# Gathering eight chosen slots by indirect DMA in place of a masked product over all 512 slots

## What is computed

```python
query = h @ Wq.T                              # h: layernorm of x, 64 numbers a token
rq, rk = query @ Wr.T, aux_keys @ Wr.T
router_scores = rq @ rk.T / sqrt(48) + log_rel           # 512 slots
top_scores, top_idx = top_k(router_scores, 8)
attn = (query . aux_keys[top_idx]) / sqrt(64) + log_rel[top_idx]
w = softmax(attn)
aux_out = (sum_k w_k * aux_values[top_idx_k]) @ Wvd.T @ Wvu.T
return h + gate * aux_out                     # gate: a sigmoid of an uncertainty
```

## Time and profile before

| what | value |
|---|---|
| median of 3 runs | 1070.32 us (1070.15 to 1070.88) |
| the profiled execution | 1074.47 us |
| its span, first to last instruction | 1072.6 us |
| TensorE busy | 97% of the span |
| VectorE, ScalarE, GpSimd busy | 74%, 52%, 17% |
| mean granted TensorE clock | 0.987 of full speed |

### The profile page before, as it was taken

One profiled execution on the slowest core, in us unless ns is written; L12 is line 12 of the kernel. 1 busy time (PEld: TensorE's weight loads), 2 busy tenths in 40 slices (PEclk: granted clock), 3 DMA queues, 4 the chain that ended last, 5 costly groups with the idle time before them and its releaser, 6 DMA issues. The chain is left out here.

```text
span 1072.6 us, 19294 instructions
## 1 busy us (share of the span) xinstructions
PE 1041.0 (97%) x6778; PEld 997.1 (93%) x6778; DVE 791.6 (74%) x1841; ACT 561.6 (52%) x881; POOL 183.4 (17%) x355
## 2 busy tenths in 40 slices
PE   6998999999999999999999999999999996999997
PEld 6998999998999999999999999999999995888885
DVE  4889646366758787787777787786877777788785
ACT  3643678544635545454554545454554554555553
POOL 0007000000002222313232222312232231000000
PEclk9999899999999999999999999999999997999999
DMA  8555557689379864744354734347352527999999
GB/s 241 157 155 193 196 212 291 246 295 280 94 219 242 218 176 117 214 110 125 92 142 115 196 98 123 112 112 214 98 142 79 151 62 228 402 409 412 403 422 371
DMA packets 109617, 218.96 MB, mean 204 GB/s; under 512 B 48388, under 2 KB 64804, under 8 KB 95528
## 3 DMA queue, kind: packets, MB, share of 16 engines
q1 hardware_dynamic: 99784, 180.68, 55.8%
q10 hardware_dynamic: 9216, 33.56, 7.9%
q0 software_dynamic: 576, 4.19, 0.9%
HBM read 174.10 MB, written 54.79 MB: 213 GB/s over the span
## 5 line engine op out<-in xcount | busy, mean ns | idle before, releaser
L56 PE MATMUL tk_bank<-b_weights,k_turned 128*128 128x384 f32 (+2 forms) x1056 | 348.8, 330 | 1.5 <-DVE b_weights L889 1.4
L58 PE MATMUL tk_bank<-b_weights,k_turned 128*128 128x384 f32 (+2 forms) x1056 | 339.9, 322 | 0.0
L57 PE MATMUL tk_bank<-b_weights,k_turned 128*128 128x384 f32 (+2 forms) x1056 | 339.7, 322 | 0.0
L56 PEld LDWEIGHTS tk_bank<-b_weights,k_turned 128*128 128x128 f32 x1056 | 198.6, 188 | 4.7 <-DVE b_weights L889 1.6
L57 PEld LDWEIGHTS tk_bank<-b_weights,k_turned 128*128 128x128 f32 x1056 | 198.8, 188 | 1.3
L58 PEld LDWEIGHTS tk_bank<-b_weights,k_turned 128*128 128x128 f32 x1056 | 198.3, 188 | 0.0
L1487 DVE STREAM_TRANSPOSE tk_bank<-k_rows 128x512 f32<-128x512 f32 x128 | 133.7, 1069 | 9.1 <-DMA k_rows<-in_x_dram 8.9
L1273 ACT ACTIVATE k_turned<-tk_bank 128x512 fp32r<-128x512 f32 x124 | 71.2, 594 | 73.9 <-DVE tk_bank L1487 73.5
L1897 DVE TENSOR_TENSOR late_x<-late_x,ob_out 128x512 f32<-128x512 f32 x96 | 65.8, 688 | 24.0 <-PE ob_out L58 22.6
L1497 DVE TENSOR_TENSOR k_turned<-tk_bank,k_turned 128x512 fp32r<-128x512 f32 x124 | 79.8, 686 | 0.9
L56 PE MATMUL tk_bank<-k_turned,a_T 128*128 128x256 f32 x256 | 76.1, 297 | 4.4 <-DVE a_T L343 3.9
(11 more groups left out here) (259 smaller groups left out, 2262.0 us busy)
## 6 DMA issues: line engine op xcount, KB each, us to landing
k_rows<-in_x_dram SPq DMA_DIRECT2D x40, 1024.0 KB, 4.8
k_rows<-in_x_dram SPq DMA_DIRECT2D x128, 256.0 KB, 5.2
late_x<-in_x_dram SPq DMA_DIRECT2D x24, 1024.0 KB, 8.3
out_dram<-late_x ACTq DMA_DIRECT2D x48, 512.0 KB, 14.1
k_rows<-in_Wq_dram SPq DMA_DIRECT2D x16, 1024.0 KB, 4.9
k_rows<-in_Wk_dram SPq DMA_DIRECT2D x9, 1024.0 KB, 4.8
out_dram<-k_rows ACTq DMA_DIRECT2D x16, 512.0 KB, 11.4
k_rows<-in_Wk_dram SPq DMA_DIRECT2D x28, 256.0 KB, 5.3
```

The lines of the kernel that those rows point to most:

```text
L56: pe.matmul(out, lh, rh, start=start, stop=False, skip_group_check=skip)
L57: pe.matmul(out, lh, rl, start=False, stop=False, skip_group_check=skip)
L58: return pe.matmul(out, ll, rh, start=False, stop=stop, skip_group_check=skip)
```

## The change

The masked row of 512 goes, with its exponential, its transposes, its product by `av` and the 512 key-dot columns of `late_route`. In their place `late_slots` ends with `max_index`, which gives eight indices per token. POOL gathers for each of the eight (`gather`, L1431) one row of 193 numbers per token out of a table in HBM (128 value numbers, 64 key numbers, the log relevance), with an indirect DMA of 128 rows. VectorE multiplies the gathered keys by the query and sums (`slot_dots`), ScalarE takes eight exponentials and scales the eight value rows (`slot_exp`, `slot_weigh`), VectorE adds them up (`slot_sum`). The table is written in the preparation. Four of the eight DMAs stand ahead of `first_mean`, four behind it. The iteration's order on VectorE also changes: `turn_x(t+1, 0)` moves ahead of `late_scale`, and `late_slots` ahead of `turn_x(t+1, 3)`; the polynomial of the activation moves to ScalarE. The slots of the last two tiles are finished in the output block, whose load into the buffer shared with the gathered rows waits for `z_out`.

```diff
 def load_slots(sp, io, scr, keep):
...
+    sp.dma_start(scr["table"][:, VB:VB + BOT], io["aux_keys"]).then_inc(keep["table_in"], 16)
+    sp.dma_start(scr["table"][:, VB + BOT:ROW], io["log_rel"].rearrange("(n a) -> n a", a=1),
+                 allow_slow_non_contiguous=True).then_inc(keep["table_in"], 16)
...
+def slot_dots(dve, keep, t, u):
+    rows = keep["slot_rows"][u].rearrange("p (k r) -> p k r", r=ROW)
+    own = rows[:, :, VB:VB + BOT]
+    query = keep["query_of"][u].unsqueeze(1).broadcast_to([P, TOPK, BOT])
+    dve.wait_ge(keep["gathered"][u], 16 * TOPK * (t // 2 + 1))
+    dve.tensor_tensor(own, own, query, ALU.mult)
+    dve.drain()
+    dve.tensor_reduce(keep["slot_dots"], own, AX.X, ALU.add)
+    dve.drain()
+    dve.scalar_tensor_tensor(keep["slot_scores"], keep["slot_dots"], -1.0 / float(BOT) ** 0.5,
+                             rows[:, :, VB + BOT:ROW].rearrange("p k o -> p (k o)"), ALU.mult, ALU.subtract)
+    dve.drain()
+    dve.tensor_reduce(keep["slot_max"], keep["slot_scores"], AX.X, ALU.min).then_inc(keep["nearest"], 1)
+def slot_weigh(act, keep, t, u):
+    act.wait_ge(keep["slot_exp"], t + 1)
+    for k in range(TOPK):
+        values = rows[:, k, 0:VB]
+        ins = act.activation(values, values, ACT.Copy, scale=keep["slot_weights"][:, k:k + 1])
+def slot_sum(dve, keep, t, u, late=False):
+    dve.wait_ge(keep["weighed"], t + 1)
+    dve.tensor_tensor(values[:, 0:4, :], values[:, 0:4, :], values[:, 4:8, :], ALU.add)
+    dve.drain()
+    dve.tensor_tensor(values[:, 0:2, :], values[:, 0:2, :], values[:, 2:4, :], ALU.add)
+    dve.drain()
+        dve.tensor_tensor(z, values[:, 0, :], values[:, 1, :], ALU.add).then_inc(keep["z_out"], 1)
...
 def late_route(t):
-                for bank_, n in ((psR, 0), (psS, NSLOT)):
-                    pe.matmul(bank_[:], qS[:], rs1[:, n:n + NSLOT], start=True, stop=False)
-                    ins = pe.matmul(bank_[:], q2s[0:BOT + 2, :], rs2[:, n:n + NSLOT], start=False, stop=True)
-            def late_turn_w(t):
-            def late_z(t, last=False):
+                pe.matmul(psR[:], qS[:], rs1[:], start=True, stop=False)
+                pe.matmul(psR[:], q2s[0:BOT + 2, :], rs2[:], start=False, stop=True).then_inc(S["routed"], 1)
...
@@ POOL
+            def gather(t, u, ks):
+                if ks[0] == 0:
+                    pool.drain()
+                    pool.wait_ge(S["slots"], t + 1)
+                    past(pool, keep["z_out"], t - 1)
+                    pool.tensor_tensor(issued[:], keep["eps"][:], keep["eps"][:], ALU.mult)
+                for k in ks:
+                    pool.indirect_dma_start(keep["slot_rows"][u][:, k * ROW:(k + 1) * ROW], None, scr["table"][:, :],
+                                            bass.IndirectOffsetOnAxis(ap=picked[u][:, k:k + 1], axis=0)
+                                            ).then_inc(keep["gathered"][u], 16)
             def tile(t, u):
                 late(t - 1, 1 - u)
                 keep_att(t, u)
-                if not last:
-                    first_mean(t + 1, 1 - u)
+                gather(t - 1, 1 - u, range(4))
+                first_mean(t + 1, 1 - u)
+                gather(t - 1, 1 - u, range(4, TOPK))
                 late_keep(t - 1, 1 - u)
-                if not last:
-                    first_rstd(t + 1, 1 - u)
+                first_rstd(t + 1, 1 - u)
...
             scales()
-            pool.wait_ge(S["hidden"], t + 1)
-            pool.tensor_tensor(hw, hid, keep["wu2"][:], ALU.mult).then_inc(S["hw"], 1)
+            gather(t - 1, 1 - u, range(TOPK))
+            gather(t, u, range(TOPK))
@@ VectorE
-            def late_slots(t):
+            def late_slots(t, u):
                 dve.wait_ge(S["routed"], t + 1)
-                dve.memset(wmax[:], OUT_OF_RANGE)
+                dve.memset(keep["slot_dots"], 0.0)
                 dve.max(top8[:], psR[:])
                 dve.drain()
-                dve.match_replace(picked, top8[:], psR[:], PICKED)
...
+                dve.max_index(picked[u][:], top8[:], psR[:]).then_inc(S["slots"], 1)
...
+            def tile(t, u, j, second=False):
                 late_stats(t - 1, 1 - u, (j if u else j - 1) // 4, second)
+                turn_ready(t + 1)
+                turn_x(t + 1, 0)
                 late_scale(t - 1, 1 - u)
+                turn_x(t + 1, 1)
                 late_q_lo(t - 1)
+                x_lo(t + 1, 1 - u, 0)
+                x_lo(t + 1, 1 - u, 1)
+                if not second:
+                    slot_dots(dve, keep, t - 2, u)
                 soft_scores(t, u, j // 4)
+                turn_x(t + 1, 2)
                 soft_att(t, u, second)
+                late_slots(t - 1, 1 - u)
+                turn_x(t + 1, 3)
+                if not second:
+                    slot_sum(dve, keep, t - 2, u)
+                x_lo(t + 1, 1 - u, 2)
+                x_lo(t + 1, 1 - u, 3)
                 att_lo(t)
                 late_learned(t - 1, 1 - u)
```

More of the change, by code:

```diff
@@ L799, in tensor @@
         turn_values(0)
-        pe.wait_ge(slot_kept, 5)
-        for t in range(4):
-            ins = pe.transpose(ps_slots[:, t * P:(t + 1) * P], ak2[:, t, :], ident[:])
-        ins.then_inc(slot_ps, 1)
         for g in range(GROUPS):
@@ L1256, in _ @@
             pe.wait_ge(S["cw_padded"], 1)
-            tile(0, 0, late=False, late_z_too=False, first=True, j=0)
-            tile(1, 1, late_z_too=False, second=True, j=0)
+            tile(0, 0, late=False, first=True, j=0)
+            tile(1, 1, second=True, j=0)
             for u in range(2):
@@ L1315, in squares, with tile @@
                                accum_out=rsq[u][:]).then_inc(S["squares"], 1)
-            def tile(t, u, late=True, late_z_too=True, last=False):
+            def tile(t, u, slots=True, last=False):
                 if last:
@@ L1364, in _ @@
             att_hi(0)
-            tile(1, 1, late_z_too=False)
+            tile(1, 1, slots=False)
             for u in range(2):
@@ L1470, in _ @@
             tile(TILES - 2, 0)
-            tile(TILES - 1, 1, last=True)
             t, u = TILES - 1, 1
+            late(t - 1, 1 - u)
+            keep_att(t, u)
+            late_keep(t - 1, 1 - u)
             pool.drain()
@@ L1747, in _ @@
             att_lo(0)
-            tile(1, 1, 0, late_z_too=False, second=True)
+            tile(1, 1, 0, second=True)
             for u in range(2):
@@ L1761, in _ @@
             late_q_lo(t - 1)
-            late_poly(t - 1)
+            slot_dots(dve, keep, t - 2, u)
             soft_scores(t, u, BATCH - 1)
             soft_att(t, u, False)
-            late_z(t - 2)
-            late_slots(t - 1)
+            late_slots(t - 1, 1 - u)
+            slot_sum(dve, keep, t - 2, u)
             att_lo(t)
```

256 lines of the change are left out of this document (108 added, 148 removed).

## The result

The changed kernel takes 1365.7 us (median of 4 runs, 1360.1 to 1366.4) against 1070.3: a ratio of 1.275, 95% interval 1.271 to 1.278. It is 295 us slower. The forecast was 1152 with a range of 1055 to 1250: the direction was right, the size far too small.

The account below looks back on a forecast made before the run. TensorE bounds the loop at 18.5 us a tile; after the change POOL's ring would, at 21.2. Thirty iterations +81, block end +2, last tile -1, preparation -1: 1070.3 + 81, about 1152 us, range 1055 to 1250.

Parts of the forecast that it names:

- What TensorE loses: Token loop: slot-weight transposes, the `av` product and two `late_route` matmuls go, together 1.7 us a tile.
- The load of `blocks`: Single buffer reloaded between a tile's fourth `turn_x` and the next tile's first: 11.5 + 7.5 = 19.0 us a tile.
- The POOL ring: From `rstd2` through query, slots and POOL's gathers to the next `rstd2`: 13.6 + 8G, 21.2 us a tile.
- eight gathers 8G: POOL's share: eight indirect DMAs a tile, G being POOL's time for one, taken as 0.95 us.
- then `first_rstd` and `rstd2`: [...] 2.1: POOL's two steps behind the gathers, from 836.00 to 838.40 less 0.3 idle: 2.1 us.
- The landing: Gathered bytes land some 2 to 4 us after issue, ahead of `slot_dots` in the next tile.
- The end of the block: Last sixteen gathers, 16 x 0.95 = 15.2 us, bring POOL to 907.5 before the output block starts: +2 us.
- Both rings hidden: Rival: POOL's ring and the load of `blocks` stay hidden, so the kernel gets faster, say 1042 us; chance 0.19.
- The load binds: Rival: G below 0.68, so the load of `blocks` sets the period at 19.0 us; 1087 us; chance 0.16.
- Locked gathers: Rival: VectorE's `slot_sum` and `late_learned` hold up gathers, 2 us a tile; about 1210 us; chance 0.13, shared with falling clock.
- A falling clock: Rival: TensorE, idle some 4 us of each 21, loses clock; about 1210 us; chance 0.13, shared with locked gathers.
- What would show it: Profile signs: `first_mean` period, L1431 mean 0.95, TensorE idle about 4 us a tile, POOL busy some 12.5 us.

Follow-up runs that it names:

- late2_none: `late2` without the gathers of tiles 2 to 28, so the selection is left out; 1105.2 us.
- none: The changed kernel without the gathers of tiles 2 to 31, all waits, drains and the marker kept; 1134.3 us.
- no_drain_b: The changed kernel with POOL's drains in the loop replaced by a semaphore raised by POOL's own instruction; 1237.8 us.
- extra: The kernel before plus eight unused indirect DMAs a tile (16 bytes an index), POOL's drains replaced by semaphores; 1082.9 us.
- wait_landed: `no_drain_b` with POOL waiting in `first_rstd`, at the first drain's place, for the eight gathers to have landed; 1340.2 us.
- late2: `late` with `slot_sum` at the tile's end, `slot_dots` back between the transposes, gathers split 2, 3 and 3; 1129.8 us.
- late3: `late2` with seven gathers ahead of `first_mean` and one behind it; 1115.3 us.
- late: The changed kernel with POOL's drains replaced as in `no_drain_b`, gathers issued one tile later and used a tile after that; 1135.4 us.
- narrow: The changed kernel with gathers from tile 2 on reading 256 bytes an index instead of 772, drains kept; 1346.1 us.
- extra_drain: `extra` with POOL's drains left as they were; 1214.3 us.

## Why the prediction was wrong

- **What TensorE loses: the right sign, and worth nothing.** No run isolates the 1.7 us. The nearest is `late2_none` at full clock: TensorE is busy for 17.5 us a tile (252.96 / 276 x 19.14) where it was 18.7. The gain couldn't show, since something else bound: in the changed kernel TensorE is busy for 194.65 us of the stretch where it was 275.87.
- **The load of `blocks`: the right mechanism, the size too small.** "11.5 + 7.5 = 19.0" measured 12.2 + 8.15 in `none`, period 20.6; +15 us should have been +64. It was the forecast's floor, and in `none` it does bind. In the changed kernel the first `turn_x` waits for its load too (100.0 us in all), but `late_scale` behind it then still waits for `rstd2`, so that wait is off the ring.
- **The POOL ring: the right ring, and its fixed part of 13.6 us holds** to 0.2 us in `no_drain_b` (in one tile: 10.7 us from `rstd2` to the next marker, where 10.55 was forecast, and 12.5 from the marker to `rstd2`, where 3.0 + 8 x 1.25 = 13.0 stands). Two terms of POOL's share failed. The first is "eight gathers 8G": the record of a gather was forecast at 0.95 and is 0.95, though 0.95 was only the middle of two bounds, so that this agrees is luck; and POOL's time for one is the distance between starts, 1.25. That is 2.4 us a tile, some 72 us. The second, and the larger, is "then `first_rstd` and `rstd2`: [...] 2.1": its drains were priced at what they cost in the earlier trace rows, where no DMA is ahead of them. Behind the gathers the same instructions take 5.87 us (614.21 to 620.08), and the drains cost 3.9 us a tile, 117 us in the loop. The first alone would have stayed in the range ("G = 1.3"; `no_drain_b` is at 1238); the second was in none of its cases. With the end of the block below, 72 + 117 + 28 = 217 us stand against the 214 that the forecast lacked.
- **The emission.** The Trainium skill, in DMA: Bandwidth & Descriptors (Latency and other measured facts), puts the first byte of a DMA on this path at about 1 us and ascribes that to the emission. The record of 0.95 agrees; the spacing of 1.25 is more.
- **The landing.** "2 to 4 us after issue" was used only to ask whether `slot_dots` would wait. In `no_drain_b` a gather lands 2.8 to 9.4 us after its issue, median 5.5, and it is this time that the drain puts into the ring.
- **The end of the block: "+2" was 30.** From the last `first_mean` to the end takes 30 us more, 28 of them beyond the forecast. Sixteen gathers need 20 us instead of 15.2, and between the two halves stands `gather`'s own drain, which waits 8.88 us. TensorE idles 28.3 us before its first transpose of the output block, against 4.53:

```profile
1167.97 0.95 POOL L1431 DMA_INDIRECT k_rows<-scratch_table,tk_picked  x1 [0.30 <-issue]
1177.80 0.19 POOL L1429 TENSOR_TENSOR tk_issued<-k_eps 128x1 f32<-128x1 f32 x1 [8.88 <-issue]
...
1187.21 0.94 POOL L1431 DMA_INDIRECT b_slot_rows<-scratch_table,tk_picked  x1 [0.30 <-issue]
```

- **Small costs on VectorE and ScalarE: near enough.** `slot_dots` takes 1.85 us (1.8 forecast), the index search 0.69 plus 0.09 (0.77). ScalarE's eight scaled copies take 2.44 us, not 1.6.
- **The rivals.** *Both rings hidden* is out: even without gathers the period is 20.6. *The load binds* describes `none`. *Locked gathers* is out here: of 256 records the median is 947 ns and the longest 1385, 12 us more in all than at the median. The Trainium skill has that lock in SBUF — State Buffer (SBUF: two separate sides); this trace leaves room for at most 0.4 us of it on one gather. *A falling clock* did come (0.81), the rival's total of 1210 was still too low, and the mechanism was not it: with the clock at 0.89 in `no_drain_b` and 0.81 in the changed kernel, the formula of POOL's ring gives both periods within 0.2 us. The lower clock goes with TensorE's waits and rose when only POOL's drains were taken away, so it is a result of the ring here and not its cause.
- **"What would show it"** named the right four signs; POOL busy for 12.5 us a tile was right too (130.24 / 276 x 27.3 = 12.9). TensorE's idle time before the query's transpose was 8 us a tile (242.7 / 30), not 4. What it lacked was POOL's idle time. The sign of its second case, a wait of the first `turn_x` for the load, came too, but beside the others, so it didn't tell the cases apart.

## What to carry to other kernels

On POOL, in every run here, a drain behind an issued DMA was a wait for the transfer; other engines were not tried. Before DMAs are moved to an engine, go through the drains that stand behind them in program order and replace those on a ring by a semaphore on the engine's own instruction; here that alone was worth 128 us of 1366. Price an instruction in a ring by the distance between starts, and place the issues where the engine would only wait, not between two results that a ring passes on: eight a tile cost 11 us in `extra` and 104 on POOL's ring. And when work is dropped from the engine that bounds, first count the second ring at the same precision as the gain: 1.7 us a tile were to be won, and the new order with VectorE's added work, without any gather, lost 1.9.

## What was unexpected in the hardware

- A drain on POOL waits for the DMAs that POOL issued, direct (5.7 us) or indirect: 3.8 with 772 bytes an index, 3.3 with 256, 4.4 with 16, and 4.0 for four instead of eight. It is not in proportion to what is moved. Compute on POOL isn't held up: without the drain the next instruction starts 0.27 us after the one before.
- An indirect DMA of 128 indices occupies POOL for 1.25 us, of which 0.30 lies outside its record; a direct one of the same size for 0.55. Bytes per index (16, 256, 772) don't change it.
- In the kernels whose drains are gone, one gather is now and then held up before it starts, where 0.30 us is usual. Counted through the run it is the 114th and the 226th, whatever the period: 1.16 and 1.15 us in `no_drain_b`, 1.17 and 1.15 in `wait_landed`, 5.15 and 1.99 in `late2`, 3.29 and 1.99 in `late3`; in `extra` the 114th and 227th, 3.16 and 3.09; in `late` only the 226th, 2.10. The 114th of `late2`, with the gather before it:

```profile
613.56 1.04 POOL L1001 DMA_INDIRECT k_rows<-scratch_table,b_picked  x1 [0.16 <-issue]
619.75 0.95 POOL L1001 DMA_INDIRECT k_rows<-scratch_table,b_picked  x1 [5.15 <-issue]
```

In the changed kernel, in `narrow` and in `extra_drain`, which drain in every tile, no gather is held up for more than 0.5 us. `wait_landed` waits for every tile's transfers and has the hold-up all the same, so it isn't the number under way at once. The fixed distance of 112 gathers, in kernels with periods of 18.85 to 26.6 us, speaks against a chance meeting with an instruction of VectorE. The cause stays open.
